# Attention with P turned in 32x32 blocks on VectorE and PV computed in eight 32x64 TensorE tiles

## The reference

```python
x = x + attn(_layernorm(x))
# inside attn:
x = _layernorm(resid_stream, ln_w, ln_b)
q = einsum('bsd,hde->bshe', x, W_q) + b_q      # k and v alike
scores = einsum('bqhe,bkhe->bhqk', q, k) * scale
scores = where(causal, scores, -inf)
pattern = softmax(scores, axis=-1)
z = einsum('bhqk,bkhe->bqhe', pattern, v)
attn_out = einsum('bqhe,hed->bqd', z, W_o) + b_o
```

## Time and profile before

| what | value |
|---|---|
| time, median of 3 runs (lowest to highest) | 1330.94 us (1328.23 to 1332.27) |
| time of the profiled execution, its span | 1327.09 us, 1325.4 us |
| PE busy | 1259.4 us, 95% |
| DVE busy | 816.3 us, 62% |
| ACT busy | 820.3 us, 62% |
| POOL busy | 302.8 us, 23% |

### The profile page before, as it was taken

One profiled execution on the slowest core, in us unless ns is written; L12 is line 12 of the kernel. 1 busy time (PEld: TensorE's weight loads), 2 busy tenths in 40 slices (PEclk: granted clock), 3 DMA queues, 4 the chain that ended last, 5 costly groups with the idle time before them and its releaser, 6 DMA issues.

```text
span 1325.4 us, 26554 instructions
## 1 busy us (share of the span) xinstructions
PE 1259.4 (95%) x7404; PEld 855.9 (65%) x7404; DVE 816.3 (62%) x2230; ACT 820.3 (62%) x1749; POOL 302.8 (23%) x311
## 2 busy tenths in 40 slices
PE   2899999999999999999999999999999997899995
PEld 1666666667666676676667777666777675445552
DVE  6666666666666666666666666666666676556563
ACT  3756666666666666666666666666666656476664
POOL 3322222222222222222222222222222201012323
PEclk8999999999999999999999999999999998999998
DMA  8866555555555555555555555555555551000000
GB/s 199 207 138 136 130 127 131 131 131 130 128 127 127 127 127 127 127 127 127 127 126 127 127 127 124 127 127 127 127 127 127 127 127 37 9 9 8 16 8 24
DMA packets 78983, 148.68 MB, mean 112 GB/s; under 512 B 41328, under 2 KB 52592, under 8 KB 67056
## 3 DMA queue, kind: packets, MB, share of 16 engines
q1 hardware_dynamic: 78960, 148.41, 49.0%
HBM read 43.21 MB, written 4.46 MB: 36 GB/s over the span
## 4 chain that ended last, share of the span: by engine, by line
PE 80%; DVE 6%; issue 5%; SPq 3%; ACT 2%; DMA 2%; POOL 1%; DVEq 0%; ACTq 0%; POOLq 0%
PE Z L517 19%; PE TB L504 15%; PE SPS L494 10%; PE SPS L495 8%; PE MB L480 8%; PE MB L525 4%; PE MB L485 4%; PE Z L641 2%; PE SPS L633 2%; DVE SSB L849 2%; PE TB L625 1%; PE MB L659 1%; SPq L367 1%; DVE ZN L798 1%; PE SPS L598 1%
## 5 line engine op out<-in xcount | busy, mean ns | idle before, releaser
L849 DVE CUSTOM_DVE_ANT_0 SSB<-SPS,MASK 128x640 f32<-128x640 f32 (+7 forms) x512 | 385.4, 753 | 311.2 <-PE SPS L495 302.7
L1115 ACT ACTIVATE PR<-SSB,NM 128x640 f32<-128x640 f32 (+7 forms) x512 | 394.3, 771 | 109.7 <-DVE NM L849 104.2
L504 PE MATMUL TB<-IDENT,PR 128*128 128x128 f32 x2304 | 349.9, 275 | 17.5 <-ACT PT L780 7.8
L504 PEld LDWEIGHTS TB<-IDENT,PR 128*128 128x128 f32 x2304 | 272.7, 141 | 102.2 <-issue 42.9
L780 ACT ACTIVATE PT<-TB 128x512 f32<-128x512 f32 (+3 forms) x384 | 205.0, 534 | 180.5 <-PE TB L504 180.5
L494 PE MATMUL SPS<-KH,QS 128*128 128x512 f32 (+2 forms) x768 | 313.7, 408 | 2.6 <-DVE NM L849 1.3
L517 PE MATMUL Z<-PT,V 128*64 128x512 f32 (+3 forms) x1536 | 269.3, 492 | 0.0
L495 PE MATMUL SPS<-KL,QS 128*128 128x512 f32 (+2 forms) x768 | 261.5, 348 | 0.0
L395 POOL CAST RH<-RAW 128x512 fp32r<-128x512 f32 x124 | 75.5, 609 | 772.0 <-ACT RAW L1077 769.1
L782 DVE COPY PT<-TB 128x128 f32<-128x128 f32 (+3 forms) x384 | 186.3, 485 | 76.2 <-PE TB L504 76.2
L517 PEld LDWEIGHTS Z<-PT,V 128*64 128x64 f32 x1536 | 101.7, 136 | 141.7 <-issue 132.3
(11 more groups left out here) (157 smaller groups left out, 880.3 us busy)
## 6 DMA issues: line engine op xcount, KB each, us to landing
KH<-RH SPq DMA_DIRECT2D x62, 512.0 KB, 8.6
KL<-RL SPq DMA_DIRECT2D x62, 512.0 KB, 9.1
XTB<-xt_scratch SPq DMA_DIRECT2D x32, 512.0 KB, 4.0
RSB<-rcp_scratch SPq DMA_DIRECT2D x128, 128.0 KB, 2.8
QS<-RH SPq DMA_DIRECT2D x31, 512.0 KB, 4.4
QS<-RL SPq DMA_DIRECT2D x31, 512.0 KB, 6.6
WQK<-in_W_q SPq DMA_DIRECT2D x33, 64.0 KB, 1.9
WQK<-in_W_k SPq DMA_DIRECT2D x33, 64.0 KB, 2.1
```

The source lines that it names most:

```text
L504: last = pe.transpose(TB[idx % 2][:, k * P:(k + 1) * P], PR[n % 4][:, (j0 + k) * P:(j0 + k + 1) * P], IDENT[:, :])
L849: v.tensor_tensor_reduce(out=SSB[n % 2][:, 0:w], in0=SP_[n % 2][:, 0:w], in1=MASK[:, S - w:S], scale=1.0, scalar=BIG, op0=ALU.add, op1=ALU ...
L1115: act.activation(PR[n % 4][:, 0:w], SSB[n % 2][:, 0:w], ACT.Exp, bias=NM[:, col:col + 1], scale=-1.0, accum_out=L[:, col:col + 1]).then_in ...
```

## The change

P is no longer turned on TensorE. VectorE turns each unit with one instruction that transposes every 32x32 block in place (`dve_turn`). Partition group i (32 partitions) then holds queries 32i to 32i+31 of the tile as columns, and 32 keys as partitions. So PV contracts over 32 keys at a time, and the four partition groups hold four different sets of queries. A matmul now has 32 rows (keys) and 64 columns (a head's z). Four partition groups times two heads make eight tiles of 32x64 of the array. Group i writes to PSUM bank i of the new tensor ZB. V must stand in all four partition groups for that: it goes to DRAM once, and eight DMAs bring it back as VR.

```diff
+        def dve_turn(v, it, n):
...
+            v.wait_ge(exp_done, it * UNITS + n + 1)
+            if n % (UNITS // 2) == 0:
+                wait(v, pv_done[n // (UNITS // 2)], it)
+            v.transpose(turned_of(n), exps_of(n)).then_inc(turned, 1)
...
-            for h in range(2):
-                last = pe.matmul(Z[h * DH:(h + 1) * DH, off:CH], V[par][:, j, h * DH:(h + 1) * DH], PT[g][:, h, j, off:CH],
-                                 start=(j == 0), stop=(j == nj - 1))
...
+            for kt in blocks:
+                if kt == 0:
+                    pe.wait_ge(turned, it * UNITS + (g + 1) * UNITS // 2)
+                    pe.wait_ge(v_early, (it + 1) * 4 * DMA)
+                if kt == TC:
+                    pe.wait_ge(v_late, (it + 1) * 4 * DMA)
+                c0 = g * P + max(kt - g * TC, 0) * TR
+                for j in range(P // TR):
+                    for i in range(P // TR):
+                        rows = slice(i * TR, (i + 1) * TR)
+                        for h in range(2):
+                            last = pe.matmul(ZB[h * DH:(h + 1) * DH, i, c0:(g + 1) * P], VR[rows, j, kt, h * DH:(h + 1) * DH],
+                                             turned_block(g, h, kt, j, rows), start=(kt == 0 and j == 0),
+                                             stop=(kt == (g + 1) * TC - 1 and j == P // TR - 1))
```

The halves of q and k are now written by GpSimd where the scores read them. That leaves two DMAs for each half of the sequence instead of six for the whole, and makes four GpSimd instructions of 64 partitions out of two of 128:

```diff
+            q, k = RAW[0:DH, s, :], RAW[DH:P, s, :]
+            q_high, k_high = QS[par][0:DH, h, part], KH[par][DH:P, h, part]
...
+                gp.tensor_copy(q_high, q).then_inc(rounded, 1)
+                gp.tensor_copy(k_high, k).then_inc(rounded, 1)
...
+            gp.tensor_tensor(QS[par][DH:P, h, part], q, q_high.bitcast(F32), ALU.subtract).then_inc(split_done, 1)
+            gp.tensor_tensor(KL[par][DH:P, h, part], k, k_high.bitcast(F32), ALU.subtract).then_inc(split_done, 1)
...
+        def store_v(sp, it, par):
+            sp.wait_ge(v_evac, it * 2 + 2)
+            sp.dma_start(v_dram[par], V[:, :, :].rearrange("p t c -> p (t c)")).then_inc(v_stored[par], DMA)
...
+            sp.wait_ge(v_stored[par], (half + 1) * DMA)
+            wait(sp, pv_done[1], it)
+            src = v_dram[par].rearrange("(j k) (t c) -> k j t c", k=TR, c=P)
+            for tiles, landed in ((slice(0, TC), v_early), (slice(TC, QT), v_late)):
+                for i in range(P // TR):
+                    sp.dma_start(VR[i * TR:(i + 1) * TR, :, tiles, :], src[:, :, tiles, :]).then_inc(landed, DMA)
```

The rest follows from this. v's bias is folded into b_o once, so v is copied out of PSUM by ACT without an addition. The output of W_o is copied out by ACT too and added to x by GpSimd. The four PSUM banks that were TB0, TB1, Z and MB are one tensor ZB now; PV, q and k, v and the output use them in turn. Both halves of PV of a step are now done in the next step. In the new order of PE:

```diff
+            scores(2, 3)
+            values(0, 0, 1, 2, 3)
+            scores(4, 5)
+            values(1, 0, 1)
+            scores(6)
+            values(1, 2, 3)
+            scores(7, 8)
+            values(1, 4, 5, 6, 7)
+            scores(9, 10)
```

More of the change, by code:

```diff
@@ L842, in f_norm_scale, with dve_mask @@
             v.reciprocal(FRS[:, FNORM[i]], FSD[:, FNORM[i]]).then_inc(f_rs, 1)
-        def dve_slot(v, it, half, par, first, last, n):
+        def dve_mask(v, it, par, n):
             w = (n // 2 + 1) * P
@@ L862, in dve_slot, with dve_step, mask, turn @@
-            if n == 9:
-                dve_reciprocal(v, it, 0, par)
-            if n in (14, 15) and not last:
-                dve_v(v, it + 1, 1 - par, n - 14)
-            if last and n == 0:
-                v.wait_ge(v_evac, STEPS * 2)
+        def dve_step(v, it, half, par, first, last):
+            def mask(n):
+                dve_mask(v, it, par, n)
+            def turn(*units):
+                for n in units:
+                    dve_turn(v, it, n)
+            def turn_back(n):
+                if not first:
+                    dve_turn(v, it - 1, n)
+            def stats(n):
+                if last:
+                    if n == 1:
+                        v.wait_ge(out_evac, (STEPS - HP) * 2 + 1)
+                    f_norm_stats(v, range(3 * n - 3, 3 * n))
+            mask(0)
+            if last:
@@ L880, in dve_slot @@
-            if last and 1 <= n <= 8:
-                if n == 1:
-                    v.wait_ge(out_evac, (STEPS - QT) * 2)
-                f_norm_stats(v, range(3 * n - 3, 3 * n))
+            turn_back(13)
+            mask(1)
+            turn_back(14)
+            mask(2)
+            turn_back(15)
+            if not first:
+                dve_reciprocal(v, it - 1, 1, 1 - par)
+            mask(3)
+            if not first:
+                dve_zn(v, it - 1, 0)
+            stats(1)
+            mask(4)
@@ new lines, in dve_step @@
+            turn(0, 1)
+            stats(2)
+            mask(5)
+            turn(2, 3)
+            stats(3)
+            mask(6)
+            turn(4, 5)
+            stats(4)
+            mask(7)
+            turn(6, 7)
+            dve_reciprocal(v, it, 0, par)
+            stats(5)
+            mask(8)
+            if not first:
+                dve_zn(v, it - 1, 1)
+            stats(6)
+            mask(9)
+            turn(8)
+            stats(7)
+            mask(10)
+            turn(9)
@@ L1241, in chunk @@
                 if not last:
[L1242 removed]
+                    turn_of(c + 2)
                 experts(c)
```

639 lines of the change are left out of this document (341 added, 298 removed).

## The result

The changed kernel takes 1576.9 us (median of four runs, 1572.5 to 1598.0), the kernel before 1329.6 (1327.6 to 1332.3). The ratio is 1.185, 95% interval 1.180 to 1.189: 18% slower, where 1204 us and "faster" were predicted. The longest of the four runs, 1598.0, was in a slower state of the chip, and the ratio leaves it out. The profiled execution has a span of 1576.8 us.

A forecast was written before the change was run, and what follows sets the result against it. PE's work was taken as the bound. A step of 26.1 + 2.0 + 1.5 = 29.6 us against 33.8 saves 130 us, the end adds 3: 1327 - 130 + 3 = 1200, predicted as 1204 us; range 1145 to 1500.

The forecast's parts named there:

- What stays, 17.7 us a step: PE's scores, q, k, v and output, left of 33.8 us without transposes (7.9) and PV (8.2).
- PV in tiles, 8.4 us: PV on PE: 9216 columns a step, all eight tiles together, 7.7 us, with four entries 8.4.
- The upper end of 21.1: PV's upper bound: 768 weight loads a step, row groups one after another, 0.055 us each, 21.1 us.
- Turns on DVE: 16 block transposes over 9216 columns on DVE, 12.6 us a step; DVE then has 25.1 us.
- DVE at half rate: Rival, 7%: DVE's transposes at half rate make it the bound at 34.3 us a step, 1350 us.
- ACT, POOL, DMA: Other engines: ACT under 20 us a step, POOL 17.6 and covered, V's way over DRAM covered by over 10.
- What holds PE and DVE together, 2.0 us: DVE's in-order wait for PV, then PE's for the last masks: 28.1 us, 2.0 above PE's own sum.
- Instructions, 1.5 us: PE's longer loop may be fetched again, six packets a step during PV, mostly hidden: 1.5 us a step.
- The rival with this name: Instruction supply, 14%: a packet takes 2.7 us or more, steps of 34 to 36 us, 1334 to 1400 us.
- The end, 3 us longer (0 to 8): Last step's turns and PV of both halves stand before the seam: 3 us more, 0 to 8.
- The sum: A step of 26.1 + 2.0 + 1.5 = 29.6 us, 4.2 less than 33.8; in all 1204 us.
- The page on the store: Skill page: PE holds 2048 instructions, 128 KiB, refilled in 16 KiB blocks; the new loop is refetched each round.

The follow-up runs named there:

- the last held kernel (joined, tuned3): Joined kernel in its last order (turns earlier, PV one score tile later), TensorE looping over single steps with constant q, k and transposed x: 1270.9 us (0.955).
- twelve pieces: Changed kernel with PV's matmuls only reordered, in pieces of 32 between score tiles 2 to 12 (64 behind the last): 1515.4 us (1.139).
- a held loop of the changed kernel: Changed kernel with TensorE looping over single steps (1742 instructions) and constant q, k and transposed x: 1633.7 us (1.231).
- the joined kernel: Changed kernel with PV's two halves of queries joined, 256 matmuls a step instead of 384: first 1682.8 us (1.268), in its last order 1347.8 (1.013).
- 1947: Instructions in a loop round of the changed kernel with half of PV's keys left out: 1298.8 us (0.978).
- a written-out program: TensorE's program without the loop: changed kernel 1581.4 us against 1576.9; joined kernel 1361.0 against 1351.7, in its last order 1345.6 against 1347.8.

## Why the prediction was wrong

- *What stays, 17.7 us a step.* Right. In the last held kernel (joined, tuned3) PE is busy 28.6 us a step, less 10.5 of PV: 18.1.
- *PV in tiles, 8.4 us.* The slope was right (0.82 ns a column over eight tiles at once), the step "the columns have to pass, so that is the time" was wrong. Passes of up to 128 columns start 10 to 15 ns apart, where the prediction had 11 on average and 3 for the narrowest, and PV without stops takes 12.9 us in twelve pieces, about 11.2 in the four of the changed kernel: 2.8 us a step too few. The upper end of 21.1, from full-width weight loads, was too high. The Trainium skill's "TensorE: Matmul & The Clock Gate" (Back-to-back issue gap) has a floor of about 25 ns between starts. For these packed tiles it does not hold: 10.2 ns were measured on average at 32 columns, and 6 to 7 between neighbours of one eight.
- *Turns on DVE.* Right: 1240 ns at 1024 columns and 288 at 128 (predicted 1.26 us and 0.31), DVE 24.7 us a step for 25.1. DVE at half rate is refuted.
- *ACT, POOL, DMA.* Right: POOL 17.7 us for 17.6, and it stays covered. V's way is covered in the changed kernel; it was DVE's turned tiles that came late once PV was joined.
- *What holds PE and DVE together, 2.0 us.* Not to be seen in the changed kernel, since PE was slower than this; in the held joined kernel PE waits 2.2 us a step for masks.
- *Instructions, 1.5 us.* This is the step that failed. The mechanism, the packets ("13.4 a round"), even the sign (gaps in PV with PE idle for nothing, some 200 packets) were in the prediction, but "six at 2 us are 12 us against 8.4 of PV and 3 of scores between, so most is hidden" was wrong. A block takes 3.3 to 3.5 us, not 2. 256 instructions of PV are used up in 1.3 to 1.9 us, as the prediction had it (1.4), but they come in rows of up to 512, so nothing lies between to hide the next block. I had spread six packets evenly over all of PV and its scores, had taken the price from data transfers (64 KB in 1.9 us), which says nothing of how soon the next block is asked for, and had given no price to the clock. Measured in place of the 1.5: 5.5 us a step of stops in PV and 1.8 at the branch, and slow matmuls behind them. The rival with this name had 34 to 36 us a step; it was the right rival and still too cheap.
- *The end, 3 us longer (0 to 8).* Too little: from the last mask on it is 13 us longer. PV stops there as well, and TensorE has a new wait of 7.0 us for DVE behind it. That the first step became 7 us shorter, which the sum did not have, hides half of it.
- *The sum.* Predicted 4.2 us a step won, measured 7.9 lost. Of these 12.1, PV's pace is 2.8, what stays 0.4, and 8.9 are stops, waits and half clock beyond the 3.5 of coupling and supply. In all 12.4 of the 41.7 us go to them: 8.7 are idle time of both PE rows (5.5 in PV, 1.8 at the branch, 1.4 elsewhere), and the rest, 3.7, is by difference the lower clock. How much of it the supply alone costs was to be measured with a held loop of the changed kernel, and that loop was not held; it is shown in the joined kernel only, 2.6 us a step. (Two slips in the prediction's working change nothing: by its own sum, steps of 28 us give 1154 and not 1151, and steps of 34 us give 1340 and not 1334.)
- *The page on the store.* The Trainium skill's "Runtime: NRT & Kernel Launch" (Instruction fetch mechanics) gives 2048 instructions and a stall at branches. That the loop is fetched again and that TensorE stands at the branch is confirmed (241 packets, 4.97 us in the median). But loops of 1742 and 1947 were refetched too, and a written-out program saves nothing of what the branch costs.

## What to carry to other kernels

Count the engine's instructions, not only its columns: where a loop is longer than what was held (here somewhere between 1228 and 1742 instructions on TensorE) and 256 of them last less than about 3.5 us, the fetch is the bound, and many stops also cost clock. Small tiles multiply instructions; give each as many columns as its output bank takes, and put long matmuls between them. When a wait is taken away and the time stays, look for the stops and waits that grew instead.

## What the hardware showed that I had not expected

- Instruction blocks came one after another, hardly ever nearer than 3.3 us, with half the DMA traffic as with all of it (3.28 and 3.34 at the shortest twentieth), in a loop and in a straight program. TensorE goes on 2.4 us after a packet's start, and the next packet starts 1.1 us later.
- A straight program of 56,312 loads and matmuls is as fast as its loop, and where instructions are sparse (18 us a block) refetching costs nothing: 1330.7 against 1328.9 us.
- Eight tiles of 32x64 do work at once: passes of 256 columns start 25.6 ns apart on average, so eight together take 0.20 us, what 256 columns at 0.83 ns take (0.21). Narrow ones don't gain in proportion: 10.2 ns at 32 columns.
- POOL's conversions take the same time on 64 partitions as on 128: 612 and 609 ns a cast.
